# The opening of a four-layer graph kernel: weights of later layers prepared among the work of the first two graphs

## The reference

```
h = relu(LN(x)); x = x + L0(h)     # 12 heads of 32; scores + beta*adj, masked where adj <= 0
h = relu(LN(x)); x = x + L1(h)     # one directed layer ("single")
h = relu(LN(x)); x = x + L2(h)     # two directed layers ("lower", "upper")
h = relu(LN(x)); x = x + L3(h)     # 12 heads, scores + adj, output projection Wo
directed layer:  a = softmax(h h^T / sqrt(384)) * adj;  a = a / (rowsum(a) + 1e-10)
                 c = (a above diagonal) @ (h Wl^T + bl) + diag(a) * (h Ws^T + bs)
                     + (a below diagonal) @ (h Wr^T + br)
                 relu(LN(c) * gain + offset)
```

## Time and profile before

| | |
|---|---|
| median of 3 runs | 2525.0 us (2524.7 to 2525.45) |
| the profiled execution | 2528.0 us, its span 2526.3 us |
| busy: PE, DVE, ACT, POOL | 2353.9, 1981.3, 1778.4, 1635.4 us |
| granted TensorE clock, mean | 0.972 of full speed |
| loads and stores by DMA | 165.39 MB, mean 65 GB/s |

### The profile page before, as it was taken

The page is one execution under the profiler, slowest core; times in us unless marked ns, Lnnn a source line. Parts: engine busy times, 40 slices in busy tenths (PEclk is TensorE's granted clock), DMA queues, the critical chain, the costliest instruction groups (busy, mean ns, idle before and its releaser), DMA issues.

```text
span 2526.3 us, 80379 instructions
## 1 busy us (share of the span) xinstructions
PE 2353.9 (93%) x26817; PEld 1741.8 (69%) x26817; DVE 1981.3 (78%) x8945; ACT 1778.4 (70%) x4412; POOL 1635.4 (65%) x2196
## 2 busy tenths in 40 slices
PE   2259999999999999999999999999999999999985
PEld 1146777777777777777777777777777777777753
DVE  4557788888887878888878888878888888888873
ACT  2336777777777777777777777777777777777763
POOL 1026777677766766777677767766777677767762
PEclk8579999999999999999999999999999999999996
DMA  3311333233223332223232323232322223322321
GB/s 102 105 51 39 69 66 70 60 72 63 69 62 66 65 71 58 67 65 73 58 66 65 74 59 68 65 68 62 64 66 71 62 64 66 71 62 64 63 53 35
DMA packets 479851, 165.39 MB, mean 65 GB/s; under 512 B 413392, under 2 KB 479440, under 8 KB 479440
## 3 DMA queue, kind: packets, MB, share of 16 engines
q1 hardware_dynamic: 479440, 160.25, 28.6%
HBM read 46.92 MB, written 12.58 MB: 24 GB/s over the span
## 4 chain that ended last, share of the span: by engine, by line
PE 82%; POOL 3%; issue 3%; DMA 2%; DVE 1%; ACT 0%; SPq 0%; DVEq 0%; POOLq 0%; ACTq 0%
PE bank L148 20%; PE bank L150 20%; PE bank L149 20%; PE bank L1360 4%; PE bank L1298 4%; PE bank L1347 2%; DMA pT<-p 2%; PE bank L1252 1%; PE bank L1314 1%; PE bank L1316 1%; PE bank L1315 1%; PE bank L1405 1%; PE bank L1403 1%; PE bank L1402 1%; POOL p L587 1%
## 5 line engine op out<-in xcount | busy, mean ns | idle before, releaser
L148 PE MATMUL bank<-w_hi,dir_hT_hi 128*128 128x384 f16 x1728 | 564.7, 327 | 0.0
L149 PE MATMUL bank<-w_lo,dir_hT_hi 128*128 128x384 f16 x1728 | 564.3, 327 | 0.0
L150 PE MATMUL bank<-w_hi,dir_hT_lo 128*128 128x384 f16 x1728 | 564.1, 326 | 0.0
L587 POOL TENSOR_TENSOR p<-probs,p 128x512 f16<-128x512 f32 x384 | 447.1, 1164 | 133.8 <-ACT p L699 133.1
L692 ACT ACTIVATE probs<-minus_scores,minus_max 128x128 f32<-128x128 f32 x1536 | 488.1, 394 | 63.1 <-DVE minus_max L909 63.1
L148 PE MATMUL bank<-hT_hi,w_hi 128*128 128x128 f16 x2304 | 412.6, 220 | 0.7 <-DVE hT_lo L895 0.7
L149 PE MATMUL bank<-hT_lo,w_hi 128*128 128x128 f16 x2304 | 412.5, 220 | 0.0
L150 PE MATMUL bank<-hT_hi,w_lo 128*128 128x128 f16 x2304 | 412.4, 220 | 0.0
L909 DVE CUSTOM_DVE_ANT_0 minus_scores<-bank,minus_score_bias 128x128 f32<-128x128 f32 x1536 | 343.5, 286 | 23.7 <-issue 13.4
L595 POOL TENSOR_TENSOR raw_weights<-raw_weights,gain_offset 128x384 f32<-128x384 f32 x192 | 191.9, 999 | 166.4 <-ACT raw_weights L779 166.4
L149 PEld LDWEIGHTS bank<-w_lo,dir_hT_hi 128*128 128x128 f16 x1728 | 169.5, 98 | 112.5 <-issue 1.2
(11 more groups left out here) (164 smaller groups left out, 7250.0 us busy)
## 6 DMA issues: line engine op xcount, KB each, us to landing
x<-in_x SPq DMA_DIRECT2D x64, 192.0 KB, 2.6
dir_adj_tile<-in_adj SPq DMA_DIRECT2D x192, 64.0 KB, 2.1
out<-raw_weights SPq DMA_DIRECT2D x64, 192.0 KB, 2.2
adj_tile<-in_adj SPq DMA_DIRECT2D x128, 64.0 KB, 2.1
pT<-p SPq DMA_TRANSPOSE x384, 2.8
raw_weights<-in_L_gnn_Wq SPq DMA_DIRECT2D x2, 576.0 KB, 4.2
raw_weights<-in_L_gnn_Wk SPq DMA_DIRECT2D x2, 576.0 KB, 5.6
raw_weights<-in_L_gnn_Wv SPq DMA_DIRECT2D x2, 576.0 KB, 6.4
```

What stands on the lines that cost most here:

```text
L148: pe.matmul(out, stat[0], move[0], start=first, stop=False)
L149: pe.matmul(out, stat[0], move[1], start=False, stop=False)
L150: return pe.matmul(out, stat[1], move[0], start=False, stop=last)
L587: pool.tensor_tensor(p16[:, c, 1, :, :], probs[:, HC * c:HC * c + HC, :], p16[:, c, 0, :, :], ALU.subtract).then_inc(p_lo[c], 1)
```

## The change

Rounds -2, -1 and 0 and `more_weights` are replaced by a list of calls written out for each engine; `run_rounds` now covers rounds 1 to 66. There are nine places for raw matrices and a tenth tile for Wo (`raw_out`), so W0, W1, the first half of W2 and Wo are all issued ahead of any wait. W2 is now two sets of three matrices, `W2` and `W2_upper`; W2_upper takes W1's places, and the rest of W3 takes the places of W2. The loads of a set's matrices and of its vectors count on semaphores of their own, and beta and v's bias on further ones. The scales and splits of the later sets stand between pieces of graphs 0 and 1. To make room, `left_hi`/`left_lo`, `x3` and the turned attention output lie inside the raw tiles from now on.

```diff
-FIRST_ROUND, LAST_ROUND = -2, G - 1 + 3
+OPENED, LAST_ROUND = 1, G - 1 + 3
...
-        raw = sb("raw_weights", [P, 6, C, D])
+        raw = sb("raw_weights", [P, 9, C, D])
+        raw_out = sb("raw_weights_of_out", [P, C, D])
...
                 dve.wait_ge(self.loaded, self.all_loaded)
                 for g, (ms, bs) in enumerate(self.groups):
                     for m, k in enumerate(ms):
-                        last = dve.tensor_reduce(amax[:, g, m:m + 1], self.raw[:, k], AX.XY, ALU.max, apply_absolute_value=True)
+                        last = dve.tensor_reduce(amax[:, g, m:m + 1], self.raw[k], AX.XY, ALU.max, apply_absolute_value=True)
+                dve.wait_ge(self.vectors_loaded, self.all_vectors)
...
                 for n, (k, c) in enumerate(self.work):
-                    if n >= 3:
-                        pe.wait_ge(w_lo_ready, self.n_split + n - 2)
+                    pe.wait_ge(w_lo_ready, self.n_split + max(n - 2, 0))
...
-        leftv = [sb(f"left_{a}", [P, D], F16) for a in ("hi", "lo")]
+        leftv = [over_raw(D // 2).bitcast(F16) for _ in ("hi", "lo")]
...
                 load_x(Task(ATTENTION, "first", 0))
-                W0.load(sp)
-                W1.load(sp)
-                run_rounds(sp, step, {0: more_weights})
+                sp.dma_start(raw_beta[:, :], ins["L0_gnn_beta"].partition_broadcast(P)).then_inc(beta_loaded, 16)
+                W0.load_vectors(sp)
+                W0.load_matrices(sp)
+                att_load_adj(first[0])
+                W1.load_matrices(sp)
+                W1.load_vectors(sp)
+                W3.load_matrices(sp, slice(3, 4))
+                W2.load_matrices(sp)
+                sp.dma_start(v_bias[:, :], ins["L0_gnn_bv"].partition_broadcast(P)).then_inc(v_bias_loaded, 16)
+                load_x(first[1])
+                W0.ready(sp)
+                W2.load_vectors(sp)
+                turn_probs(first[0], 0)
...
+                W1.ready(sp)
+                W2_upper.load_matrices(sp)
+                W2_upper.load_vectors(sp)
+                dir_load_adj(single[0])
+                load_x(first[2])
+                W2.ready(sp)
+                W3.load_matrices(sp, slice(0, 3))
+                W3.load_vectors(sp)
...
             @block.gpsimd
...
+                W1.find_largest_of_all(pool)
+                probs_lo(first[0], 0)
+                W2.find_largest_of_all(pool)
+                probs_lo(first[0], 1)
+                probs_lo(first[0], 2)
...
             @block.scalar
...
+                norm_context(single[0])
+                W2_upper.bias_rows_high(act, bias_rows, [(8 + m, m, 0) for m in range(3)])
+                W2_upper.split_high(act)
+                v_hi_split(first[1])
+                exponents(first[1], 2)
+                probs_hi(first[1], 2)
+                W3.split_high(act)
...
             @block.vector
...
+                att_stats(first[0])
+                att_mean_var(first[0])
+                att_var_eps(first[0])
                 W0.find_scales(dve)
                 dve.tensor_scalar(q_unscale[:, 0:1], unscale[:, 0:1], -float(HD ** -0.5), None, ALU.mult).then_inc(setup, 1)
+                dve.wait_ge(w_kept_by_pool, 1)
+                drop_masked(first[0])
+                score_bias(first[0])
+                att_turned_lo(first[0])
...
+                W1.find_scales(dve)
+                biased_max(first[0], 0)
+                biased_max(first[0], 1)
+                biased_max(first[0], 2)
+                W2.find_scales(dve)
+                att_stats(first[1])
...
+                W1.split_low(dve)
+                row_sums(first[0])
+                row_scales(first[0])
+                attended_rows(first[0])
+                W2.bias_rows_low(dve, bias_rows, [(5 + m, m, 0) for m in range(3)])
+                W2.split_low(dve)
+                dir_stats(single[0])
...
+                mask(single[0])
+                W2_upper.find_scales(dve)
+                left_lo(single[0])
...
+                W3.find_scales(dve)
...
+                denominator(single[0])
+                right_lo(single[0])
...
+                W2_upper.split_low(dve)
+                att_stats(first[2])
+                att_mean_var(first[2])
+                v_lo_split(first[1])
+                att_var_eps(first[2])
+                add_to_x(single[0])
+                turned_bias(dve)
+                W3.split_low(dve)
+                sum_out_bias(dve)
+                drop_masked(first[2])
+                dir_stats(lower[0])
...
+                W3.ready(dve)
+                run_rounds(step)
...
             @block.tensor
...
+                project_v(first[0])
+                W1.turn(pe)
+                attend(first[0], 0)
+                attend(first[0], 1)
+                attend(first[0], 2)
+                att_turn_h(first[1])
+                W2.turn(pe)
...
+                combine(single[0])
+                pe.wait_ge(d["ctx_ready"], 1)
+                W2_upper.turn(pe)
+                turn_v_bias(pe)
+                W3.turn(pe)
+                project_v_bias(pe)
+                W3.ready(pe)
+                dir_turn_h(lower[0])
```

More of the change, by code:

```diff
@@ L273, in _source @@
             def _source(self, n, k, c):
-                return banks[n % 3][:, 0:D] if self.transposed else self.raw[:, k, c]
+                return banks[n % 3][:, 0:D] if self.transposed else self.raw[k][:, c]
             def split_low(self, dve):
@@ L415, in build @@
         LAST, ONLY_FIRST = ("last",), ("first",)
+        first, last = ([Task(ATTENTION, kind, graph) for graph in range(4)] for kind in ATTENTION.kinds)
+        single, lower, upper = ([Task(DIRECTED, kind, graph) for graph in range(4)] for kind in ("single", "lower", "upper"))
         def is_last(t):
@@ new lines, in _ @@
+                W1.bias_rows_low(dve, bias_rows, [(2 + m, m, 0) for m in range(3)])
+                W1.split_low(dve)
[5 more added lines that the diff above has]
+                dir_stats(single[0])
+                att_turned_lo(first[1])
+                dir_mean_var(single[0])
+                dir_var_eps(single[0])
@@ L1236, in _ @@
+                row_scales(first[1])
+                minus_row_max(lower[0])
+                attended_rows(first[1])
+                mask(lower[0])
+                left_lo(lower[0])
+                W3.ready(dve)
+                run_rounds(step)
             @block.tensor
@@ L1358, in project @@
                 def project(t, part, bank, ready):
-                    weights, w = WEIGHTS[t.kind], PART[t.kind] + part
+                    weights, w = WEIGHTS[t.kind], part
                     pe.matmul(bank[:, 0:D], first_and_33rd[:, :], bias_rows[:, ROW[t.kind] + part, :], start=True, stop=False)
```

241 lines of the change are left out of this document (164 added, 77 removed).

## The result

| | before | changed |
|---|---|---|
| median us | 2525.01 (four runs beside it) | 2495.22 (2494.39 to 2495.8, four runs) |
| ratio | | 0.9883, interval 0.9868 to 0.9898 |
| profiled execution: time, span | 2528.0, 2526.3 | 2495.49, 2493.4 |
| mean granted clock | 0.972 | 0.975 |
| VectorE begins round 1 | 181.51 | 153.92 |

The change gains 29.8 us. The forecast was 50 (2475 us, range 2464 to 2490), so the direction was right and the size outside the range. I read the changed kernel's trace in the order of the forecast. First three windows: the opening up to round 0, from there to round 1, and both together (length, then busy us and instructions of TensorE's matmuls and loads, VectorE, ScalarE and GpSimd, then clock, DMA share, GB/s).

A forecast was written before the change was run, and what follows sets the result against it. VectorE's waits in the opening were taken to set round 1's start, the rest following one for one: 66.3 + 63.6 + 0.9 = 130.8 against 181.6 us, so 50.8 gained; median 2474.2 plus 0.8 for hops, 2475 us, range 2464 to 2490.

The forecast's parts named there:

- Part 2: W1's scales beside graph 0's q and k: hidden by a wait for TensorE, cost 0 or 0.8 us, maxima end at 37.4.
- parts 3: W2's first half and W1's split between pieces of graphs 0 and 1: no load wait, round 0 starts at 66.3 us.
- 4: Round 0 with W2's upper half and W3 prepared inside: grows from 31.5 to 63.6 us, both loads hidden.
- late hop: Allowance of 0.9 us in the whole opening for VectorE's long waits for GpSimd's maximum, such as the 2.2 us one.
- part 1: Opening to the end of W0: 7.3 us saved, W0 ends at 27.2, moving bias loads ahead of the matrices costs nothing.
- The cover that I named: Parts 2 and 3 have real cover: W1's scales hide in a wait for TensorE; later W2 and W3 loads are hidden.
- The two doubts: TensorE's clock in the opening, some 4 us either way, left at 0; VectorE rows slowed beside GpSimd's, 0 to 5.8 us.
- upper bound of 2490: Nothing runs beside anything; only load waits of 18.0 and 10.0 us and part 1's 7.3 go, a gain of 35.
- The second rival: New order serialises: weight blocks make TensorE, ScalarE and GpSimd wait in turn at left_lo, right_lo, graph 0's attention; 2490 us, chance 0.20.
- The third: Gain given back in rounds 1 to 4, bound by something unmoved such as loads; 2500 to 2524 us, chance 0.02.
- the fourth: Slower: new places inside raw weight tiles lengthen each round, VectorE held up behind GpSimd; 2538 us, chance 0.03.

The follow-up runs named there:

- exp. 2: Changed kernel with each partition taking its own largest value for W1, both halves of W2 and W3, no all-reduce there; 2475.88 us.
- exp. 6: Changed kernel with all five maxima found by TensorE and VectorE instead of GpSimd, and W0's matrices issued ahead of its biases; 2474.41 us.
- experiment 5: Changed kernel with layer 0's three weight matrices issued ahead of its bias vectors, as before the change; 2492.66 us.
- experiment 9: Kernel of exp. 6 with TensorE taking W1's maximum ahead of graph 0's scores instead of behind them; 2472.05 us.
- experiments 1: Changed kernel with all five maxima over partitions found by TensorE and VectorE instead of GpSimd's all-reduce; 2477.45 us.
- 7: Kernel of exp. 6 with the first maximum, that of W0, left to GpSimd; 2476.66 us.

## Why the prediction was wrong, step by step

The bound was read rightly: what this change is worth is the shift of one point. In the forecast it moved to 130.8, it moved to 153.45 + 0.56 = 154.0; the 23.2 us between them, less the 5.2 by which the rest came out shorter, are nearly the 18.3 that the profiled time, 2495.49, lies above the 2477.2 of my sum. (TensorE's row stands at 9 from the fourth slice, about 190 us, and not from the seventh as I wrote; nothing hung on it.) The points of the sum:

| | forecast | changed | exp. 2 | exp. 6 |
|---|---|---|---|---|
| last low half of W0 ends | 27.2 | 30.0 | 30.1 | 27.2 |
| graph 0's maxima end | 37.4 | 44.1 | 40.0 | 39.7 |
| W2's scales end | 44.2 | 56.1 | 46.9 | 47.9 |
| last low half of W1 ends | 54.5 | 65.9 | 56.7 | 57.9 |
| round 0 begins | 66.3 | 79.2 | 67.2 | 68.2 |
| from there to left_lo | 14.3 | 15.4 | 14.7 | 16.2 |
| from there to right_lo | 25.6 | 31.7 | 25.3 | 28.0 |
| left_lo of the lower layer ends | 130.8 | 154.0 | 130.8 | 133.6 |

- **Part 2 failed, and with it parts 3 and 4.** "Cost 0 or 0.8; I keep 0.9 us for this kind of late hop in the whole opening." I priced GpSimd's maximum at the 0.6 us that three hops average, and these were all-reduces behind another one or, at W0, 15.8 us behind GpSimd's last work. The one with elementwise work right in front of it, 2.2 us, I priced by the piece that VectorE happened to see. The true price was in the bracket of GpSimd's own row, 6.14 <-issue, and further up the way back, 7.06. Against the forecast W1's wait cost 3.9 us (the maxima end 6.7 late, 2.8 of it from part 1), W2's 5.2, W3's 5.0 at right_lo. W1's 3.9 needed a second cause: the change issues the bias of v behind the loads of W1, Wo and the first half of W2, and GpSimd stood 11.1 us for it, of which some 7.3 are the change back. By the rows, 21.87 + 7.3 for the way back + 1.0 + 6.3 for the way in puts that all-reduce at 36.5 instead of 40.22 had the bias been there. That is an estimate; no run issues it earlier.
- **The way back was not in the sum at all.** I let GpSimd serve W2's maximum "before the second and third low halves of the probabilities, which it finishes about 46". They began at 62.67, and graph 0's attention came out with 2.7 us of wait on VectorE: round 0 is 12.9 us late and not 11.4. The same in part 4: the last change back (7.47 us, to 117.22) put a low half of graph 1, and behind it in GpSimd's order the power of the context's norm, to 119.00; ScalarE stood 17.5 us for it, and the upper bias rows began 40.6 us after round 0 instead of 30.0. That is 4.5 us beyond the late right_lo, and the bracket of 7.50 us at VectorE's bias rows.
- **Part 1 failed by 2.8 us.** "That the two bias loads now stand ahead of the three matrices changes no sum of bytes; I cost it at nothing." The sum over all seven loads is the same, but not the bytes that must land before the last matrix: in the trace of the changed kernel the reductions wait for Wv and begin at 16.34, in experiment 5 at 12.15. Without GpSimd's changes this is worth 3.0 us; with them, nothing of it reached round 1 in the one trace there is.
- **The cover that I named held.** On VectorE no row waits for a load after the first reduction (on GpSimd one does, for the bias of v, see above), W1's scales lie beside q and k, and with the all-reduces gone (experiment 2) the first four points are late by 2.2 to 2.9 us, which is W0's late start, and the last four are within 0.9.
- **The two doubts came out near zero.** VectorE was busy for 86.75 us where it was 88.2 before, so rows beside GpSimd's cost little, and not 5.8. What can be seen is 0.4 us: three bias rows took 2.06 us at 121.48, beside a GpSimd row of 0.99 that began at 121.08, and 1.67 elsewhere. I had called the scales safe, but their small rows are not: in experiment 2 a `pow` of 0.17 us took 0.81 at 45.41, beside a low half from 45.05 to 46.21. The granted clock of the two stretches was 0.74 and 0.70, still a mixture; of one change of it in the opening I can show the price, 1.4 us (experiment 9).
- **Bound and rivals.** My upper bound of 2490, "nothing runs beside anything", did not hold: the gain was 29.8 us and not 35, since the bound left room for old costs only, and the new order made new ones. The second rival, 2490 by serialising, came near in number and was wrong in mechanism: it named left_lo, right_lo and the attention of graph 0, and these were late, but by an engine that changed its kind of work. The third (2500 or more) was as near in number and did not come, nor did the fourth: rounds 1 to 66 took 2339.5 and 2340.5 us, within what the kernel before itself shows (2336.7 and 2344.8).

What stays open: why the same kernel's rest varies by 8 us between executions, which also bounds what can be said of differences of 2 to 3 us between experiments 1, 6, 7 and 9; what an earlier bias of v would have saved; and what lowers TensorE's clock in one execution of the opening's end and not in another.

## What to carry to other kernels

Before work of one engine is interleaved, look in its own timeline for idle time whose releaser is "issue" and ask what stands on either side: here it was the engine's own cost, and it multiplied with the number of alternations, not with the work. Where a helper on that engine is needed among other work, group such calls, put them where the engine idles anyway, or do them elsewhere: four short steps over TensorE and VectorE (1.7 us from the maxima to `pow` at W0, 3.2 at W1, where TensorE still had the scores to do, 1.9 at W2) replaced all-reduces that took 13 to 14 us of GpSimd's time each with their two changes. And price a moved load by the bytes that must land before the last one waited for, not by the sum over all.

## What the runs showed that I had not expected

- GpSimd: elementwise to partition all-reduce 5.7 to 7.1 us idle, back 6.7 to 7.7 us, at every change that no longer wait covered; all-reduces in a row 0.44 us each (x3 in 1.32).
- Its first all-reduce began no earlier than 18.62 and 18.63 us, 10.6 to 10.8 us of "issue" after its last elementwise instruction, though the maxima were there at 16.9 and 17.2. The Trainium skill's 6 us (the section named above) don't cover this first wait.
- Two loads of 192 KB, each one spread over all partitions, issued ahead of three of 576 KB, moved the last of these by 4.2 us (the reductions begin at 16.34 instead of 12.15). By the bytes alone it would be 1.8 us, an estimate from experiment 5, where the three matrices took 7.9 us from the first issue (4.18) to the last landing (5.18 + 6.9). What makes up the rest is not shown.
- The same kernel before had its start of round 1 at 181.5 and 184.0 us and the rest at 2344.8 and 2336.7 in two executions, at 0.972 and 0.971 of the clock.
